# A cross-attention and mixture-of-experts block: VectorE's key and query scaling ahead of the expert choice and the places

## The reference, cut to what matters

```python
def attention(q, k, v):                                  # 16 heads of 16
    scores = jnp.einsum('bqhd,bkhd->bhqk', q, k) * scale
    return jnp.einsum('bhqk,bkhd->bqhd', jax.nn.softmax(scores, axis=-1), v)
q = rms_norm(linear(x, q_w, q_b), norm_q_w)              # x: layernorm of the input
k_img = rms_norm(linear(ctx_img, k_img_w, k_img_b), norm_k_img_w)
v_img = linear(ctx_img, v_img_w, v_img_b)
x = x + linear(attention(q, k_img, v_img), o_w, o_b)
...
logits = jnp.einsum('th,eh->te', layernorm(x), gate_w)   # 8 experts
topw, sel = jax.lax.top_k(softmax(logits), 2)            # two of them, weights made to sum to 1
out = sum over the two experts of topw * (silu(g) * u) @ w2[e]
x = x + out
```

## Time and profile before

| | |
|---|---|
| time, median of 3 runs | 529.12 us (527.29 to 530.03) |
| the profiled execution | 529.43 us |
| its span from first to last instruction | 527.7 us |
| busy in the span: PE, PEld | 428.6 us, 385.3 us |
| DVE, ACT, POOL | 389.0 us, 276.7 us, 307.1 us |
| mean granted TensorE clock | 0.937 |

### The profile page before, as it was taken

How to read it: one execution, slowest core, us unless ns; L and a number is a source line. 1 busy time by engine, 2 the same in 40 slices (tenths; PEclk the granted TensorE clock), 3 DMA queues, 4 the chain that set the end, 5 groups by cost and what they waited for, 6 DMA issues and landing times.

```text
span 527.7 us, 15112 instructions
## 1 busy us (share of the span) xinstructions
PE 428.6 (81%) x4376; PEld 385.3 (73%) x4376; DVE 389.0 (74%) x1295; ACT 276.7 (52%) x806; POOL 307.1 (58%) x530
## 2 busy tenths in 40 slices
PE   1779999999999998999999750699999999999000
PEld 1668888888878887888788640599999999998000
DVE  7447798889888988888988764376767776776384
ACT  5236566665666565656665420365656655665000
POOL 6625458787878787878788666044444444544100
PEclk9989999999999999999999975699999999999655
DMA  7242453323233333333332215433444344431599
GB/s 202 62 128 80 136 158 92 108 87 95 92 108 96 94 96 97 101 91 97 95 108 74 83 42 150 121 112 117 130 116 131 114 123 114 132 109 61 191 404 359
DMA packets 55706, 64.74 MB, mean 123 GB/s; under 512 B 9664, under 2 KB 49227, under 8 KB 55627
## 3 DMA queue, kind: packets, MB, share of 16 engines
q1 hardware_dynamic: 44170, 42.20, 27.7%
q0 software_dynamic: 6528, 16.86, 9.2%
q10 hardware_dynamic: 4928, 4.72, 2.6%
HBM read 32.86 MB, written 23.27 MB: 106 GB/s over the span
## 4 chain that ended last, share of the span: by engine, by line
PE 41%; POOL 26%; issue 13%; DVE 8%; DMA 5%; SPq 3%; ACT 2%; POOLq 1%; DVEq 0%; ACTq 0%
POOL sorted_rows L466 9%; PE bank L1122 8%; PE bank L1123 8%; PE bank L1124 8%; PE bank L1340 4%; POOL r_qk L422 4%; DMA we_l<-expert_out 4%; POOL we_l L414 4%; POOL ct_l L408 2%; POOL rstd L422 2%; POOL row L451 2%; PE bank L1369 2%; PE bank L1370 2%; PE bank L1359 1%; PE bank L1358 1%
## 5 line engine op out<-in xcount | busy, mean ns | idle before, releaser
L538 POOL DMA_INDIRECT expert_out<-probs,late x72 | 70.0, 972 | 94.1 <-ACT probs L718 91.5
L466 POOL DMA_INDIRECT sorted_rows<-row,place_i x64 | 69.3, 1082 | 33.4 <-POOL row L458 15.6
L1122 PE MATMUL bank<-we_h,xt_h 128*128 x144 | 53.2, 369 | 0.1
L1080 DVE SCALAR_TENSOR_TENSOR probs<-xn,late,bank 128x128 f32<-128x128 f32 x72 | 25.0, 348 | 34.7 <-ACT xn L706 34.2
L1123 PE MATMUL bank<-we_l,xt_h 128*128 x144 | 46.9, 325 | 0.0
L1124 PE MATMUL bank<-we_h,xt_l 128*128 x144 | 46.8, 325 | 0.0
L1072 DVE TENSOR_TENSOR xt_l<-bank,xt_h 128x256 fp32r<-128x256 f32 x72 | 30.6, 425 | 21.2 <-ACT xt_h L700 17.4
L1340 PE MATMUL bank<-ident,late 128*128 128x128 f32 x144 | 30.6, 295 | 18.4 <-DMA late<-sorted_rows 16.5
L630 ACT ACTIVATE probs<-bank 128x1024 f32<-128x1024 f32 x32 | 32.9, 1027 | 23.3 <-PE bank L1236 19.6
L706 ACT ACTIVATE xn<-bank 128x176 f32<-128x176 f32 x72 | 22.9, 318 | 41.3 <-PE bank L1124 41.3
L422 POOL TENSOR_TENSOR rstd<-veps,half_neg 128x1 f32<-128x1 f32 x64 | 36.8, 576 | 5.3
(11 more groups left out here) (198 smaller groups left out, 1593.6 us busy)
## 6 DMA issues: line engine op xcount, KB each, us to landing
late<-sorted_rows SPq DMA_DIRECT2D x72, 129.0 KB, 2.1
we_f<-w_exp SPq DMA_DIRECT2D x32, 152.0 KB, 2.4
v_bd<-v_sb SPq DMA_DIRECT2D x128, 34.0 KB
ctx_in<-ctx_t SPq DMA_DIRECT2D x32, 128.0 KB, 2.4
qp<-q_hl SPq DMA_DIRECT2D x128, 32.0 KB
we_h<-expert_out SPq DMA_DIRECT2D x8, 512.0 KB, 6.8
we_l<-expert_out SPq DMA_DIRECT2D x8, 512.0 KB, 15.7
x<-x SPq DMA_DIRECT2D x3, 1024.0 KB, 5.8
```

Of the source, the lines that this page charges most:

```text
L466: pool.indirect_dma_start(sorted_rows, bass.IndirectOffsetOnAxis(ap=place_i[:, t.slot // 2, k, t.par:t.par + 1], axis=0), row[:, k, t.slot ...
L538: pool.indirect_dma_start(expert_out, bass.IndirectOffsetOnAxis(ap=hs[:, r, D:D + 1].bitcast(U32), axis=0), y_sb[:, r % YRING, :], None, b ...
L1122: pe.matmul(dst, a_h, b_h, start=start, stop=False)
```

## The change

In VectorE's turn the block of gate_of_x, k_scale and q_scale (with the one-time fold_gate of turn 0) now stands ahead of choose and route, directly behind att_lo. No instruction is added, removed or altered, and the lists of the other engines are the same.

```diff
                 att_lo(tile(3))
+            if isinstance(j, int) and j == s == 0:
+                fold_gate()
+            if tile(0).live:
+                gate_of_x(tile(0))
+                k_scale(tile(0))
+                q_scale(tile(0))
             if s % 2 == 1 and tile(5).live:
                 a = tile(5)
                 a.first = isinstance(j, int) and a.n == 0
                 choose(a, tile(4), (s - 5) // 2 % 2)
             if s % 2 == 0 and tile(6).live:
                 route(tile(6), tile(5), (s - 6) // 2 % 2)
-            if isinstance(j, int) and j == s == 0:
-                fold_gate()
-            if tile(0).live:
-                gate_of_x(tile(0))
-                k_scale(tile(0))
-                q_scale(tile(0))
             if tile(3).live:
                 residual(tile(3))
```

## The result

| | before | changed |
|---|---|---|
| median of 4 runs each | 528.20 us | 541.71 us |
| lowest to highest | 527.18 to 530.03 | 539.57 to 545.09 |
| the profiled execution | 529.43 us | 541.02 us |
| its span | 527.7 us | 539.3 us |

The ratio is 1.0258 with a 95% interval of 1.0194 to 1.0322, that is 10 to 17 us. The forecast was 539.1 us, 10.0 us more than the 529.12 us of before then on record (with the fourth execution the median is 528.20), in a range of 533.5 to 545: the direction and the range held. The two profiled executions differ by 11.6 us.

What follows compares the result with a forecast made beforehand. GpSimd was taken to bound the attention stage. Terms of 0.4, 7.8 and 1.8 us summed to 10.0 us on the profiled 529.43 us, giving 539.4; the median lies 0.3 us lower, so 539.1 us, range 533.5 to 545.

Steps and rivals of the forecast that it cites:

- 0.43 us and 0.12 us of slack: Slack of ScalarE's squares before GpSimd's ms_eps in route turns, and of TensorE's q transpose after k_lo in choice turns.
- Choice turn: Odd turns with expert choice: k_scale no earlier, choice queued behind the r_qk wait, later VectorE work 1.26 us late.
- One sign of being wrong: No GpSimd wait for the squares, one in both kinds of turn, or a wait for L904 or the places.
- Route turn: Turns with places: k_scale ties with r_qk, residual 1.5 us late, lost in the following choice turn's wait.
- (a): Turn 5, where GpSimd is idle and waits for the squares: residual later, 0.4 us after TensorE's slack.
- (b): Choice turns 7 to 27, each followed by a GpSimd-bound route turn: 11 x 0.71 = 7.8 us.
- (c): Turns 29 to 31, with no r_qk left afterwards: VectorE's lateness counts in full, 1.8 us.
- so this stays: Turns after 31, without projections, are a chain through VectorE: the 1.8 us stays, expert stage unchanged but later.
- Absorbed: Rival, 10%: VectorE's waits absorb the lateness, GpSimd's list sets the pair, only (c) or less remains: 529 to 531.5 us.
- No recovery: Rival, 5%: the choice turn doesn't give back the lateness, each pair costs the full 1.26 us: 545 us.
- Port: Rival, 10%: VectorE-GpSimd port sharing holds up the choice by 0.28 us in 12 turns: 3.4 us more, 542.5 us.
- Faster: Rival, 4%: r_qk of choice turns ready early, scaling runs before the choice, 0.6 us earlier per pair: 522 us.

Runs made afterwards that it cites:

- the run with the weights moved: Kernel before, with the pair's three expert-weight instructions executed by VectorE instead of GpSimd, reciprocal for power: 529.61 against 530.41 us.
- the run with the places alone: Kernel before, with only the places (route) moved behind the key and query scaling, the choice staying ahead: 528.77 against 529.31 us.
- the choice alone: Kernel before, with only the expert choice moved behind the key and query scaling, the places staying ahead: 540.92 against 529.31 us.
- four extra instructions: Kernel before, order kept, with four unused statistics instructions on VectorE behind q_scale in choice turns up to 31: 541.29 against 529.31 us.
- places and half of the choice: Kernel before, with places and the choice's cast and compares behind the scaling, expert weights left on GpSimd: 533.12 against 529.86 us.
- the kernel with the ratio 0.9867: Kernel before, with expert weights on VectorE, and places and the choice's cast and compares behind the scaling: 521.16 against 528.77 us.
- The changed kernel with the weights on VectorE: The changed kernel, with the pair's expert weights also moved from GpSimd to VectorE: 532.02 us against 530.41 us of the kernel before.
- the half choice: Kernel before, with only the choice's cast and three compares (0.59 us) moved behind q_scale: 529.33 against 529.31 us.
- the single extra instruction: Kernel before, order kept, with one unused statistics instruction (0.34 us) on VectorE behind q_scale in choice turns: 530.64 against 530.41 us.

## Why the prediction was right, point by point

**The bound.** GpSimd bounds the pair: shown by its new wait alone adding to the pair, and by extra work on VectorE being free up to a threshold. But it was a bound by a hair: the run with the weights moved shows a second loop at 17.38 us behind GpSimd's 17.47, in part from the longer matmul group; with the group at its old length and the places behind the scaling it is 16.94. The prediction read the 0.43 us and 0.12 us of slack right and did not ask what the pair would be without GpSimd; for this change it did not matter.

**Choice turn.** k_scale no earlier, 0.04 us behind r_qk; VectorE idle ahead of it for 1.23 us in turn 9 (forecast 1.1 to 1.8). The 0.43 us of before that the prediction starts from belong to turn 15 with its slow cast; 0.70 to 0.73 us is what turns 9, 11, 13, 17 and 19 of before have. The sum doesn't use it. Choice 1.25 us (1.26). The gaps behind releases repeated: 0.15 us for TensorE (0.14 taken), 0.25 for GpSimd (0.25).

**GpSimd's wait.** 0.85 us in place of the usual 0.08, so 0.77 (forecast 0.71), in route turns only, none at the places, as written. The pair grew by 0.74 us, its median by 0.70. One sign of being wrong did appear, once: in turn 23 GpSimd waited 0.46 us for L904 (veps), ahead of which the prediction had left a gap of 0.14 us. The next k_scale is 9.22 us behind that of turn 23 in place of the usual 8.87, so the 0.71 us a pair had no room for it; the other ten pairs have no such wait.

**Route turn.** Costs nothing by itself: the run with the places alone.

**The sum.** Where the two profiled executions stand apart, by the start of the same event:

| event | before | changed | apart | step | forecast |
|---|---|---|---|---|---|
| att_lo of turn 5, ahead of any moved instruction | 64.84 | 63.64 | -1.20 | | |
| k_scale of turn 7 | 83.92 | 83.03 | -0.89 | +0.31 | (a) 0.4 |
| k_scale of turn 29 | 276.04 | 283.32 | +7.28 | +8.17 | (b) 7.8 |
| residual of turn 31 | 293.48 | 302.98 | +9.50 | +2.22 | (c) 1.8 |
| plan of the expert stage (L1066) | 323.15 | 334.27 | +11.12 | +1.62 | 0 |
| end of the span | 527.7 | 539.3 | +11.6 | +0.48 | 0 |

The three forecast terms gave 10.7 us for 10.0. That the whole came out so near to it is in part luck: the changed execution was 1.20 us ahead before any moved instruction had run (over the twelve profiled kernels this start lies between 61.65 and 65.39 us), and what followed turn 31 put 2.1 us on top. The step that failed is a small one, "so this stays": after turn 31 another 1.6 us were added up to the plan, where nothing was forecast. They are all in turn 32, on TensorE: its transposes of the attention (L1218) are 9.50 us apart, the projection behind the scores 11.11 (299.52 and 310.63 us). Busy time by stretch (PE, PEld, DVE, ACT, POOL, then the granted clock) of this place, before and then changed:

```profile
295.16:299.71 4.55, 3.16 (x39) 2.60 (x36) 3.74 (x14) 1.01 (x3) 3.61 (x7) 1.00 0.16 46
```

```profile
304.60:309.20 4.60, 2.95 (x20) 2.22 (x21) 3.64 (x13) 1.01 (x3) 3.68 (x7) 0.76 0.16 47
```

Before, the clock is at its full 2.4 GHz; changed, it is granted at 0.76 on the mean, since it falls to the lower level, 1.2 GHz, in the middle of the stretch; from 307 to 310 us it is 0.50. The transposes behind the wait for the maxima (L1218), first before, then changed:

```profile
297.52 0.44 PE L1218 MATMUL bank<-ident,att 128*128 128x128 f32 x2 [0.29 <-DVE att L866]
297.79 0.27 PE L1232 MATMUL bank<-qp,late 128*128 128x256 f16 x1
```

```profile
307.02 0.69 PE L1218 MATMUL bank<-ident,att 128*128 128x128 f32 x2 [0.29 <-DVE att L866]
307.50 0.42 PE L1232 MATMUL bank<-qp,late 128*128 128x256 f16 x1
```

The score matmuls of this turn take 0.42 instead of 0.27 us until the last few. TensorE's last two waits ahead of them are the same in both (1.06 and 0.29 us), but in the changed kernel a third stands just before, for the late k_lo:

```profile
295.39 0.41 PE L1155 MATMUL bank<-ident,late 128*128 128x128 f32 x2
```

```profile
304.89 0.41 PE L1155 MATMUL bank<-ident,late 128*128 128x128 f32 x2 [0.98 <-DVE late L833]
```

That this wait brings the clock down is near at hand, and the other profiles don't bear it out. From the start of L1218 to the projection behind the scores, this place takes 2.0 us in before and five other kernels, and 3.3 to 3.9 us in six: the changed one, the choice alone, four extra instructions, places and half of the choice, weights on VectorE, and the kernel with the ratio 0.9867. The changed kernel with the weights on VectorE has the same three waits (0.99, 1.06 and 0.29 us) and keeps its clock; the old order with these weights has only the last two, as before, and loses it. So the 1.6 us are the price of a fall of the clock that this order of instructions doesn't decide alone; what does stays open. The profiled executions differ by 11.6 us and the medians by 13.5; the spread of single runs (539.57 to 545.09) covers that, and which part moves from run to run is open.

**The rivals.** Absorbed: no, the half choice and the single extra instruction are where it would have held. No recovery: no, the choice turn gives the lateness back, since the sum of the halves went up by 0.74 and not by 1.26. Port: not seen; GpSimd's busy time did not grow (306.0 for 307.1 us) and the median cast stayed short:

```profile
L925 DVE CAST top_no<-top_no x16: 169/169/440, 66.1 to 327.0; 128x4 f32<-128x4 uint32 x16
```

169 ns median, 440 at most, against 170 and 449. Its slow ones start at 316.82 and 326.98 us, behind the last k_scale. By the Trainium skill's rule of the exclusive port pair ("SBUF — State Buffer", section "SBUF: two separate sides") a single slow cast may still be such a block, which no run here shows; it didn't move the sum. Faster: it needed r_qk of the choice turn earlier. The runs with the weights on VectorE provide that, and there the new order costs 2.4 us in place of 13.5; faster it isn't there either.

## What to carry to other kernels

Before an instruction is put ahead of others on an in-order engine, look at when its input arrives: an instruction that waits takes everything behind it along, and short work that stood in the wait's shadow then stands behind it, on the path. A cost like this has a threshold, the slack of the next engine down the path, so a half or a quarter of the edit can be free where the whole costs 12 us. And where two or three loops are within a few per cent of each other, a shorter list of the bound engine or a better order of the next one may gain nothing alone, as here; try them together. When a gain then comes, look whether it is the one that was meant: here 0.52 us of it in a pair of turns followed a group of matmuls that nobody had edited.

## What the runs showed of the hardware

Three things I had not expected. The gaps between a release and the start of the waiting instruction are as steady as durations: 0.24 to 0.26 us from ScalarE's sum to GpSimd's ms_eps, 0.14 to 0.15 us from VectorE's k_lo to TensorE's transpose, 0.03 to 0.05 us from GpSimd's r_qk to VectorE's k_scale, from turn 2 on and in both kernels, wherever the later instruction waits. TensorE's clock fell to the lower level in turn 32 in six of the twelve profiled kernels and cost 1.3 to 1.9 us there; two kernels with the same last waits (1.06 and 0.29 us), before and the one with the weights on VectorE, differ in it. And a group of 32 small matmuls that takes 1.07 to 1.10 us in all turns of before took 1.30 to 1.59 us in 20 of 21 turns of the kernel with the weights on VectorE, without a wait that the profile names.
